# The second reading of x by two row gathers issued from GpSimd instead of two transfers issued from SyncE

## The chip, the core and the metric

The kernel runs on one core of a Trainium2 chip. A core has five engines with queues of their own: TensorE (PE in the profile, PEld for its weight loads), VectorE (DVE), ScalarE (ACT), GpSimd (POOL) and SyncE (SP), which here only issues DMAs (SPq). They share an on-chip memory (SBUF) and an accumulator memory (PSUM), and they order each other by semaphores. The metric is the device time of one execution in microseconds (us); lower is better.

## The reference

x is 8 x 1024 x 256, float32. Four blocks are added onto it, each behind a layer norm.

```python
x = x + attn_a(_layernorm(x), ...)   # gated linear attention (16 heads), then an MLP 256-512-256
x = x + ffn(_layernorm(x), ...)      # 8 experts 256x256, top two weighted
x = x + attn_b(_layernorm(x), ...)   # recurrence h = tanh(x_t B + h A^T), 16 wide, over 1024 steps
x = x + ffn(_layernorm(x), ...)      # the same expert layer again

def attn_a(x, ...):
    h = _ln(x, ln_w, ln_b)
    ...                               # o = gated linear attention of h, normed and gated
    x = x + o.reshape(Bb, Tt, HEADS * DV) @ Wo
    h2 = _ln(x, ln_w, ln_b)
    return x + jax.nn.gelu(h2 @ W1 + b1, approximate=False) @ W2 + b2
```

The raw x is wanted twice: once at the start, for the norms, and again later, for the normed x inside attn_a (`x` there) and for the outer `x +`.

## The kernel before, in words

Time is cut into 32 rounds of 32 steps (TS). One round holds 8 batch rows x 32 steps = 256 tokens, as two tiles of 128 partitions; a token's 256 numbers lie along the partition. Work on a round is spread over eight stages: in iteration `it` of the loop, stage k works on round it - k. Eight iterations are written out at the start, then a loop over `it` from 8 to 31, then seven more for the end. Each engine has its own program in the order written out by hand in its `body(it)`, and waits on semaphores; nothing is reordered at run time.

The names that matter. `xin` is the first reading of x (stage 0), `xag` the second (stage 2). From `xag` VectorE makes `xhat` (line 881), the normed x, one tile at a time, and GpSimd makes `res` = xag + b2 in stage 3 (line 485). When `res` of a round is done, `xag` may be overwritten. GpSimd then forms `state` (line 489), adds `xmid` to `res` (line 496), writes `elast` (line 499) and, from VectorE's moments `mv_f`, makes the reciprocal standard deviation `rf` (lines 401 and 403, a power). VectorE waits for `rf` in order to make `y` from `xmid` (line 881 too; one helper). Later GpSimd adds `part` and `acc` for the expert layer (lines 431 and 433).

The recurrence runs through all engines' programs: TensorE's step (line 1271, tile `ps<-hs,aT`), ScalarE's two tanh (lines 566 and 567), VectorE's `hs` (line 858), 32 times a round, interleaved with the other work.

SyncE's program in each iteration: the spreads of v and of the scores through DRAM (`vrow`, `vx`, `arow`, `atx`), then `xin` of a new round, then `xag`, then the store of a finished round. The second reading waits only for `res` of the round before, and stands behind the spreads in SyncE's queue.

Of the kernel before, what the change touches and what calls it, by code (L numbers as in the profile page):

```python
# [8 lines left out]
U32 = mybir.dt.uint32  # L9
ALU = mybir.AluOpType  # L10
# [3 lines left out]
P = 128  # L14
B, T, D = 8, 1024, 256
# [81 lines left out]
def build(nc, x, wts, out):  # L97
    ctx = ExitStack()
    with ctx:
# [5 lines left out]
        def sem(name):  # L105
            if name not in sems:
                sems[name] = ctx.enter_context(nc.semaphore(name))
            return sems[name]
# [131 lines left out]
        REST = {w: n + 1 for n, w in enumerate(("gate", "early", "scaled_out", "late", "recurrence", "experts0", "experts"))}  # L240
        recurrence_weights = [(a_raw[m * N:(m + 1) * N, n * N:(n + 1) * N], wts["A"]) for m in range(3) for n in range(3)]
        X_FIRST = 16 * TILES * (BQ - 1)
        GATE, EARLY, LATE = (16 * len(w) for w in (gate_weights, early_sync + early_scalar, late_sync + late_scalar))
        A_LOADED = 16 * len(recurrence_weights)

        def live(it, stage):

            return not isinstance(it, int) or 0 <= it - stage < ROUNDS
# [36 lines left out]
        def past(count):  # L285

            return max(count, 0) if isinstance(count, int) else count
# [18 lines left out]
        def load_first(eng, dst, i, name):  # L306
            for q in range(BQ):
                eng.dma_start(dst[q * TS:(q + 1) * TS, i, :], x[i * BQ + q, 0:TS, :]).then_inc(sem(name), 16)

        @block.sync  # L310
        def _(sp):
            def load_x(dst, n, name):
                for i in range(TILES):
                    sp.dma_start(dst[:, i, :], x[i * BQ:(i + 1) * BQ, bass.ds(n * TS, TS), :]).then_inc(sem(name), 16)

            def store(n):
                for i in range(TILES):
                    sp.dma_start(out[i * BQ:(i + 1) * BQ, bass.ds(n * TS, TS), :], m2.acc[:, i, :]).then_inc(sem("stored"), 16)

            load_first(sp, xin, 0, "x_loaded")  # L320
            for dst, src in early_sync:
                sp.dma_start(dst, src).then_inc(sem("early"), 16)
            for i in range(TILES):
                load_first(sp, xag, i, "x_again")
            sp.wait_ge(sem("pads_zero"), 1)
            sp.wait_ge(sem("early"), EARLY)
            for dst, src in late_scalar + late_sync[:6]:
                sp.dma_start(dst, src).then_inc(sem("late"), 16)
            sp.wait_ge(sem("spread_zero"), 1)

            def spread_v():
                for h in range(HQ):
                    cols = slice(h * J * DV, (h + 1) * J * DV)
                    sp.dma_start(vx[h * TS:(h + 1) * TS, :, h, :], vrow[:, :, cols].rearrange("b s c -> s b c")).then_inc(sem("v_spread"), 16)

            def spread_scores():
                for h in range(HQ):
                    sp.dma_start(atx[h * TS:(h + 1) * TS], arow[:, :, h, :].rearrange("b s c -> s b c")).then_inc(sem("att_spread"), 16)

            def body(it):  # L340
                c0, c2, c7 = (cnt(it, k) for k in (0, 2, 7))
                if live(it, 2):
                    spread, last, written = value(sp, c2), value(sp, c2 - 1), value(sp, c2 * 16)
                    sp.wait_ge(sem("pads_zero"), 1)
                    sp.wait_ge(sem("O11"), last)
                    sp.wait_ge(sem("vt1"), spread)
                    sp.wait_ge(sem("vt0"), spread)
                    sp.dma_start(vrow.rearrange("(i q) s c -> (q s) i c", q=BQ), vtok[:]).then_inc(sem("v_out"), 16)
                    sp.wait_ge(sem("pads_zero"), 1)
                    sp.wait_ge(sem("v_out"), written)  # L350
                    spread_v()
                    masked, kept = value(sp, 2 * c2), value(sp, c2 * 16)
                    sp.wait_ge(sem("pads_zero"), 1)
                    sp.wait_ge(sem("att"), masked)
                    sp.dma_start(arow.rearrange("(i q) s h c -> (q s) i (h c)", q=BQ), att[:].rearrange("p i h c -> p i (h c)")).then_inc(sem("att_out"), 16)
                    sp.wait_ge(sem("pads_zero"), 1)
                    sp.wait_ge(sem("att_out"), kept)
                    spread_scores()
                if live(it, 0) and not (isinstance(it, int) and it == 0):
                    sp.wait_ge(sem("y0"), past(TILES * (c0 - 1)))  # L360
                    load_x(xin, it, "x_loaded")
                if isinstance(it, int) and it == 1:
                    for dst, src in late_sync[6:]:
                        sp.dma_start(dst, src).then_inc(sem("late"), 16)
                    for dst, src in recurrence_weights:
                        sp.dma_start(dst, src).then_inc(sem("a_loaded"), 16)
                if isinstance(it, int) and it == 2:
                    sp.wait_ge(sem("weights_rest"), REST["late"])
                    sp.dma_start(stage[:].rearrange("p (c e d) -> p c e d", c=KC, e=E), wts["experts"]).then_inc(sem("experts"), 16)
                if live(it, 2) and not (isinstance(it, int) and it == 2):  # L370
                    sp.wait_ge(sem("res"), past(c2 - 1))
                    load_x(xag, it - 2, "x_again")
                if live(it, 7):
                    sp.wait_ge(sem("acc2"), c7 * VECTOR_GROUPS * 2)
                    store(it - 7)

            rounds(sp, body)
            sp.wait_ge(sem("stored"), 16 * TILES * ROUNDS)


        @block.gpsimd
        def _(pool):
# [12 lines left out]
            g.memset(state[:], 0.0).then_inc(sem("pads_zero"), 1)  # L395
            pool.wait_ge(sem("pads_zero"), 1)
            pool.wait_ge(sem("spread_zero"), 1)

            def rstd(mv, buf, name, count, shift=False):

                g.tensor_scalar(buf[:, 0, :], mv[:, :, 1], EPS, 1.0, ALU.add, ALU.mult).then_inc(sem(f"var_{name}"), 1)  # L401
                pool.wait_ge(sem(f"var_{name}"), count)
                g.tensor_tensor(buf[:, 1, :], buf[:, 0, :], mhalf[:, 0:TILES], ALU.pow).then_inc(sem(f"rstd_{name}"), 1)
                if shift:
                    pool.wait_ge(sem(f"rstd_{name}"), count)
                    g.tensor_tensor(buf[:, 0, :], buf[:, 1, :], mv[:, :, 0], ALU.mult).then_inc(sem(f"mr_{name}"), 1)
                    target = value(pool, count)
                    pool.wait_ge(sem("pads_zero"), 1)
                    pool.wait_ge(sem(f"mr_{name}"), target)
                    g.tensor_scalar(buf[:, 2, :], buf[:, 0, :], -1.0, 1.0, ALU.mult, ALU.mult).then_inc(sem(f"shift_{name}"), 1)  # L410
# [24 lines left out]
            def keep_norm(count):  # L435

                pool.wait_ge(sem("rstd_inner"), count)
                pool.wait_ge(sem("xhat"), past(TILES * (count - 1)))
                g.tensor_tensor(nrm[:, 1, :], ra[:, 1, :], one[:, 0:TILES], ALU.mult)
                g.tensor_tensor(nrm[:, 0, :], mv_a[:, :, 0], one[:, 0:TILES], ALU.mult).then_inc(sem("nrm"), 1)  # L440

            def gated(count):

# [4 lines left out]
            def body(it):  # L448
# [34 lines left out]
                if live(it, 3):  # L483
                    pool.wait_ge(sem("x1"), past(c3 - 1))
                    g.tensor_tensor(res[:], xag[:], b2[:].unsqueeze(1).broadcast_to([P, TILES, D]), ALU.add).then_inc(sem("res"), 1)
                if live(it, 2):
                    pool.wait_ge(sem("smid"), c2)
                    pool.wait_ge(sem("dstate"), c2)
                    g.tensor_tensor(state[:], smid[:], dstate[:], ALU.add).then_inc(sem("state"), 1)
# [10 lines left out]
                if live(it, 3) and not filling(it):  # L500
                    target = value(pool, c3)
                    pool.wait_ge(sem("pads_zero"), 1)
                    pool.wait_ge(sem("mv_f"), target)
                    rstd(mv_f, rf, "f", c3)
                if live(it, 4):
                    pool.wait_ge(sem("scaled1"), past((c4 - 1) * 2 * TILES + 2))
                    start_acc(m1, 0, c4)
# [315 lines left out]
        def _(dve):  # L823
# [131 lines left out]
            def body(it):  # L955
# [192 lines left out]
                    split_state(15, c5)  # L1148
                if live(it, 2):
                    dve.wait_ge(sem("nrm"), c2)  # L1150
                    dve.wait_ge(sem("x_again"), c2 * 16 * TILES + X_FIRST)
                    normed(xhat, xag, nrm[:, 0, :], nrm[:, 1, :], 0).then_inc(sem("xhat"), 1)
                if live(it, 3):
                    dve.wait_ge(sem("h2T0"), c3)
# [518 lines left out]
```

## Time and profile before

| | |
|---|---|
| time, median of 2 runs | 1697.11 us (1696.15 to 1698.06) |
| span of the profiled execution, first to last instruction | 1692.7 us |
| that execution's own time | not given apart from the two runs; its span is 4.4 us under their median |
| granted TensorE clock, mean over the span | 0.974 |
| busy: TensorE, VectorE, ScalarE, GpSimd | 94%, 75%, 62%, 49% |
| one full round in the middle | 48.6 us |
| DMA | 48 GB/s over the span |

A row of a timeline has: start, duration, engine, line, operation, tile written <- tiles read, shapes, count; in brackets the idle time of the engine just before it and what ended that. Rows that follow each other closely on an engine are merged (x2, x4). Busy shares are averages: where an engine's idle time lies in a round is seen only in its timeline.

### The profile page before, as it was taken

To read this page: it belongs to the slowest core of one execution; us is meant where nothing else is said; L and a number is where in the kernel's file an instruction comes from. 1 tells how busy PE (TensorE), PEld (TensorE's weight loads), DVE (VectorE), ACT (ScalarE), POOL (GpSimd) and SP (SyncE) were. 2 spreads that over 40 slices of the span, in tenths; PEclk is the share of its full clock that TensorE was granted. 3 is DMA by queue.
4 is the path that set the end of the run, shared out by engine and by line. 5 is a ranking of instruction groups with operands and counts; after the bars stand their busy time and mean duration, and the time that the engine had idled before them with its cause. 6 is when DMAs were issued, how large, how long until landed. Compare 5 with 4: busy or idle time off the path is not lost.

```text
span 1692.7 us, 51627 instructions
## 1 busy us (share of the span) xinstructions
PE 1591.6 (94%) x16840; PEld 1324.5 (78%) x16840; DVE 1274.3 (75%) x4556; ACT 1051.2 (62%) x3851; POOL 823.1 (49%) x1294
## 2 busy tenths in 40 slices
PE   4588999999999999999999999999999999998866
PEld 3477888888888888888888888888888888887654
DVE  4566777887788778787888787887888877876544
ACT  4656666666766666666666666666666667655431
POOL 3554454554555455545454554454545545543211
PEclk7799999999999999999999999999999999999978
DMA  5211111111111111011111111111111111110000
GB/s 151 84 57 45 52 58 58 42 39 43 43 56 56 56 51 43 31 52 47 56 56 56 46 42 35 50 50 56 56 56 43 37 44 44 52 52 8 7 7 13
DMA packets 117250, 81.49 MB, mean 48 GB/s; under 512 B 42016, under 2 KB 108224, under 8 KB 117056
## 3 DMA queue, kind: packets, MB, share of 16 engines
q1 hardware_dynamic: 116208, 80.10, 15.4%
q8 instruction: 38, 0.62, 0.2%
q10 hardware_dynamic: 976, 0.54, 0.1%
q14 instruction: 28, 0.23, 0.0%
HBM read 47.06 MB, written 33.55 MB: 48 GB/s over the span
## 4 chain that ended last, share of the span: by engine, by line
PE 82%; DVE 6%; issue 3%; DMA 3%; ACT 2%; SPq 2%; POOL 1%; ACTq 0%; DVEq 0%; POOLq 0%
PE ps L1254 62%; PE ps L1260 4%; PE ps L1271 4%; PE ps L1285 2%; PE ps L1301 2%; PE ps L1442 2%; PE ps L1331 2%; DMA xag<-in_x 2%; PE ps L1321 2%; PE ps L1312 1%; DVE hs L858 1%; DVE att L947 1%; DVE dstate L1075 1%; PE ps L1292 1%; DMA arow<-att 1%
## 5 line engine op out<-in xcount | busy, mean ns | idle before, releaser
L1254 PE MATMUL ps<-we,yT 128*128 128x512 f32 x3072 | 824.5, 411 | 0.3 <-DVE h2Ts L953 0.3
L1254 PEld LDWEIGHTS ps<-we,yT 128*128 128x128 f32 x3072 | 546.5, 191 | 100.9 <-issue 1.1
L566 ACT ACTIVATE h_lead<-ps 48x8 fp32r<-48x8 f32 x1024 | 172.4, 168 | 443.8 <-PE ps L1271 430.3
L858 DVE SCALAR_TENSOR_TENSOR hs<-ps,cst,h_lead 48x8 fp32r<-48x8 f32 x1024 | 224.7, 219 | 223.8 <-ACT ps L567 216.1
L1271 PEld LDWEIGHTS ps<-hs,aT 128*128 128x128 f32 x1024 | 195.1, 191 | 126.4 <-DVE hs L858 99.1
L1271 PE MATMUL ps<-hs,aT 128*128 128x8 f32 x1024 | 215.9, 211 | 39.7 <-DVE hs L858 38.3
L890 DVE SCALAR_TENSOR_TENSOR stage<-ps,coef,stage 128x256 f32<-128x256 f32 x384 | 183.1, 477 | 13.8 <-POOL stage L433 5.0
L890 DVE SCALAR_TENSOR_TENSOR acc<-ps,coef,acc 128x256 f32<-128x256 f32 x384 | 181.7, 473 | 6.6 <-POOL acc L433 2.7
L518 POOL TENSOR_TENSOR orstd<-omean,mhalf 128x32 f32<-128x32 f32 x32 | 174.6, 5455 | 0.2
L567 ACT ACTIVATE ps<-ps 48x8 f32<-48x8 f32 x1024 | 162.8, 159 | 0.0
L431 POOL TENSOR_TENSOR part<-part 128x256 f32<-128x256 f32 x64 | 46.9, 732 | 204.2 <-ACT part L584 201.8
L431 POOL TENSOR_TENSOR stage<-stage 128x256 f32<-128x256 f32 x64 | 47.8, 746 | 187.7 <-ACT stage L584 187.7
L1254 PE MATMUL ps<-h2Ts,wa 128*128 128x256 f32 x768 | 106.9, 289 | 3.7 <-DVE h2Ts L953 3.7
L1254 PE MATMUL ps<-wa,gTs 128*128 128x256 f32 x768 | 108.1, 291 | 0.7 <-DVE gTs L953 0.6
L1254 PE MATMUL ps<-wa,hTs 128*128 128x512 f32 x384 | 103.3, 406 | 0.0
L1254 PEld LDWEIGHTS ps<-wa,gTs 128*128 128x128 f32 x768 | 96.0, 191 | 7.0 <-issue 6.0
L1254 PEld LDWEIGHTS ps<-h2Ts,wa 128*128 128x128 f32 x768 | 95.8, 191 | 5.4 <-DVE h2Ts L953 3.9
L512 POOL TENSOR_SCALAR omean<-oss 128x32 f32<-128x32 f32 x32 | 8.9, 277 | 178.5 <-DVE oss L1172 178.5
L575 ACT ACTIVATE ps<-ps,lnb,lnw 128x256 f32<-128x256 f32 x128 | 67.2, 529 | 30.5 <-PE ps L1260 30.5
L1254 PEld LDWEIGHTS ps<-wa,hTs 128*128 128x128 f32 x384 | 67.6, 188 | 14.1
L401 POOL TENSOR_SCALAR ra<-mv_a 128x2 f32<-128x2 f32 x32 | 6.1, 191 | 145.0 <-DVE mv_a L877 145.0
L606 ACT ACTIVATE qx<-qt,cst 128x256 f32<-128x256 f32 x128 | 64.4, 505 | 1.4 <-DVE qt L977 1.4
(184 smaller groups left out, 3200.4 us busy)
## 6 DMA issues: line engine op xcount, KB each, us to landing
arow<-att SPq DMA_DIRECT2D x32, 512.0 KB, 2.8
atx<-arow SPq DMA_DIRECT2D x128, 128.0 KB, 2.8
vrow<-vtok SPq DMA_DIRECT2D x32, 256.0 KB, 2.1
vx<-vrow SPq DMA_DIRECT2D x128, 64.0 KB, 2.0
out<-stage SPq DMA_DIRECT2D x64, 128.0 KB
xin<-in_x SPq DMA_DIRECT2D x62, 128.0 KB
xag<-in_x SPq DMA_DIRECT2D x62, 128.0 KB
stage<-in_experts SPq DMA_DIRECT2D x1, 2048.0 KB, 9.5
```

The costliest lines, as they stand in the source:

```text
L431: g.tensor_tensor(m.part[:, i, 0, :], m.part[:, i, 0, :], m.part[:, i, 1, :], ALU.add).then_inc(sem(f"part{m.s}"), 1)
L518: g.tensor_tensor(orstd[:], omean[:], mhalf[:], ALU.pow).then_inc(sem("orstd"), 1)
L566: a.activation(h_lead[:], ps[0:NB, BANK["RB"], k * B:(k + 1) * B], ACT.Tanh)
L567: a.activation(h_whole, ps[0:NB, BANK["RB"], k * B:(k + 1) * B], ACT.Tanh).then_inc(sem("rnn_tanh"), 1)
L575: a.activation(ps[:, bank, c * TOK:(c + 1) * TOK], ps[:, bank, c * TOK:(c + 1) * TOK], ACT.Identity, bias=lnb[:, c:c + 1], scale=lnw[:, c: ...
L606: return a.activation(qx[:, h, :, :], bt(qt[:]), ACT.Identity, scale=headmask[:, h:h + 1])
L858: v.scalar_tensor_tensor(hs[0:NB, :, k], h_whole, keeps_rest, h_lead[:].bitcast(F32), ALU.mult, ALU.subtract).then_inc(sem("rnn_h"), 1)
L890: v.scalar_tensor_tensor(m.acc[:, i, :], ps[:, bank, half * D:(half + 1) * D], m.coef[:, i, e:e + 1], m.acc[:, i, :], ALU.mult, ALU.add).t ...
L1254: ins = t.matmul(dst, left(lp, c), right(rp, c), start=(n == 1), stop=(n == 3 * chunks))
L1260: ins = t.transpose(ps[:, dst_bank, c * TOK + i * P:c * TOK + (i + 1) * P], src[:, i, c * P:(c + 1) * P], ident)
L1271: return t.matmul(ps[0:NP, BANK["RB"], k * B:(k + 1) * B], aT[:], hs[:, :, (k - 1) % TS], start=False, stop=True, skip_group_check=True)
L1285: ins = t.matmul(ps[ROUTED * g:ROUTED * (g + 1), bank, 0:TOK], rw[:, c, :], m.yT[:, part, c, :].bitcast(F32), start=True, stop=True, skip_ ...
```

## The change

SyncE no longer reads `xag`, neither in its loop (two transfers an iteration) nor at the start (eight transfers of 32 rows for round 0). GpSimd gets the numbers of the 2 x 128 rows of round 0 in a small tile `row` (four iotas; a fifth fills `row[:, 1]` with 32). In iterations 2 to 33 it issues two indirect DMAs, each gathering 128 rows of 1 KB of x by the numbers in one column of `row`; then, some instructions on, it waits for both to have landed and adds 32 to the row numbers. VectorE's wait for the landing counts from the new number.

```diff
@@ setup
+        rows_x = x.rearrange("b t d -> (b t) d")
+        row = sb("row", [P, 2, TILES], U32)
@@ SyncE
-            for i in range(TILES):
-                load_first(sp, xag, i, "x_again")
...
-                if live(it, 2) and not (isinstance(it, int) and it == 2):
-                    sp.wait_ge(sem("res"), past(c2 - 1))
-                    load_x(xag, it - 2, "x_again")
@@ GpSimd, start
+            for q in range(BQ):
+                ins = g.iota(row[q * TS:(q + 1) * TS, 0, :], [[BQ * T, TILES]], base=q * T, channel_multiplier=1)
+            ins.then_inc(sem("rows_first"), 1)
+            pool.wait_ge(sem("rows_first"), 1)
+            g.iota(row[:, 1, :], [[0, TILES]], base=TS, channel_multiplier=0).then_inc(sem("row"), 1)
...
+            def read_again(count):
+                target = value(pool, past(count - 1))
+                pool.wait_ge(sem("pads_zero"), 1)
+                pool.wait_ge(sem("res"), target)
+                pool.wait_ge(sem("row"), count)
+                for i in range(TILES):
+                    g.indirect_dma_start(xag[:, i, :], None, rows_x, bass.IndirectOffsetOnAxis(ap=row[:, 0, i:i + 1], axis=0)).then_inc(sem("x_again"), 16)
+
+            def next_rows(count):
+                target = value(pool, count * 16 * TILES)
+                pool.wait_ge(sem("pads_zero"), 1)
+                pool.wait_ge(sem("x_again"), target)
+                g.tensor_tensor(row[:, 0], row[:, 0], row[:, 1], ALU.add).then_inc(sem("row"), 1)
@@ GpSimd, body: between res and state
                     g.tensor_tensor(res[:], xag[:], b2[:].unsqueeze(1).broadcast_to([P, TILES, D]), ALU.add).then_inc(sem("res"), 1)
                 if live(it, 2):
+                    read_again(c2)
+                if live(it, 2):
                     pool.wait_ge(sem("smid"), c2)
@@ GpSimd, body: between rf and the start of acc
                     rstd(mv_f, rf, "f", c3)
+                if live(it, 2):
+                    next_rows(c2)
                 if live(it, 4):
@@ VectorE
-                    dve.wait_ge(sem("x_again"), c2 * 16 * TILES + X_FIRST)
+                    dve.wait_ge(sem("x_again"), c2 * 16 * TILES)
                     normed(xhat, xag, nrm[:, 0, :], nrm[:, 1, :], 0).then_inc(sem("xhat"), 1)
```

The order on GpSimd in the loop, from `r` of the expert layer to the first `acc`, before:

```order
L410 TENSOR_SCALAR r<-r 128x2
L485 TENSOR_TENSOR res<-xag,b 128x512
L489 TENSOR_TENSOR state<-smid,dstate 128x512
L496 TENSOR_TENSOR res<-res,xmid 128x512
L499 TENSOR_TENSOR elast<-eq,one 128x8
L401 TENSOR_SCALAR rf<-mv_f 128x2
L403 TENSOR_TENSOR rf<-rf,mhalf 128x2
L506 ISA
L431 TENSOR_TENSOR part<-part 128x256
```

and the same place now:

```order
L412 TENSOR_SCALAR r<-r 128x2
L503 TENSOR_TENSOR res<-xag,b 128x512
L451 DMA xag<-in_x,row 128x256 x2
L509 TENSOR_TENSOR state<-smid,dstate 128x512
L516 TENSOR_TENSOR res<-res,xmid 128x512
L519 TENSOR_TENSOR elast<-eq,one 128x8
L403 TENSOR_SCALAR rf<-mv_f 128x2
L405 TENSOR_TENSOR rf<-rf,mhalf 128x2
L294 ISA
L458 TENSOR_TENSOR row<-row 128x2
L528 ISA
L433 TENSOR_TENSOR part<-part 128x256
```

Two DMAs stand between `res` and `state`, and the addition to `row` between `rf` and `part`. (ISA rows are register work and waits.)

The end of SyncE's loop, from the score spread on, before:

```order
L338 DMA atx<-arow 32x8x128 x4
L360 REGISTER_ALU
L314 ISA
L314 DMA xin<-in_x 128x1x256
L314 ISA
L314 DMA xin<-in_x 128x1x256
L314 ISA
L314 DMA xag<-in_x 128x1x256
L314 ISA
L314 DMA xag<-in_x 128x1x256
L374 ISA
L318 ISA
```

and now:

```order
L338 DMA atx<-arow 32x8x128 x4
L360 REGISTER_ALU
L316 ISA
L316 DMA xin<-in_x 128x1x256
L316 ISA
L316 DMA xin<-in_x 128x1x256
L371 ISA
L320 ISA
```

The two `xag` transfers and their address work are gone; the stores (line 318, now 320) follow `xin` directly.

## Rows read from the trace of the kernel before

**Rows 1.** The page: busy time by engine, and the chain by engine

```profile
PE 1591.6 (94%) x16840; PEld 1324.5 (78%) x16840; DVE 1274.3 (75%) x4556; ACT 1051.2 (62%) x3851; POOL 823.1 (49%) x1294
...
PE 82%; DVE 6%; issue 3%; DMA 3%; ACT 2%; SPq 2%; POOL 1%; ACTq 0%; DVEq 0%; POOLq 0%
```

**Rows 2.** Windows, one full round: length, busy time by engine, clock, DMA

```profile
800.00:848.60 48.60, 48.37 (x528) 40.57 (x527) 39.24 (x143) 32.36 (x122) 25.50 (x41) 1.00 0.16 49
```

**Rows 3.** Timeline of GpSimd in a full round

```profile
813.29 0.19 POOL L410 TENSOR_SCALAR r<-r 128x2 f32<-128x2 f32 x1 [0.16 <-POOL r L406]
...
815.13 1.31 POOL L485 TENSOR_TENSOR res<-xag,b 128x512 f32<-128x512 f32 x1
816.39 1.51 POOL L489 TENSOR_TENSOR state<-smid,dstate 128x512 f32<-128x512 f32 x1
...
819.38 0.19 POOL L401 TENSOR_SCALAR rf<-mv_f 128x2 f32<-128x2 f32 x1
819.65 0.71 POOL L403 TENSOR_TENSOR rf<-rf,mhalf 128x2 f32<-128x2 f32 x1
826.10 0.72 POOL L431 TENSOR_TENSOR part<-part 128x256 f32<-128x256 f32 x1 [5.74 <-ACT part L584]
```

**Rows 4.** Timeline of all engines in the same round

```profile
818.74 0.23 DVE L877 BATCH_NORM_AGGREGATE mv_f<-st_f 128x2 f32<-128x6 f32 x2
...
820.39 0.41 DVE L881 TENSOR_SCALAR y<-xmid,mv_f,rf 128x256 f32<-128x256 f32 x1 [0.51 <-POOL rf L403]
...
820.72 0.22 DVE L858 SCALAR_TENSOR_TENSOR hs<-ps,cst,h_lead 48x8 fp32r<-48x8 f32 x1
...
821.21 0.19 PEld L1271 LDWEIGHTS ps<-hs,aT 128*128 128x128 f32 x1
...
822.63 0.20 DVE L858 SCALAR_TENSOR_TENSOR hs<-ps,cst,h_lead 48x8 fp32r<-48x8 f32 x1
...
822.89 0.19 PEld L1271 LDWEIGHTS ps<-hs,aT 128*128 128x128 f32 x1 [0.34 <-DVE hs L858]
```

**Rows 5.** Tile xag: duration ns min/median/max, first and last; waits for it

```profile
L314 SPq DMA_DIRECT2D xag<-in_x x62: 531/548/615, 64.4 to 1502.1; - x62
...
  DMA xag<-in_x: 8.6, 9
```

**Rows 6.** Timeline of SyncE's queue in the same round

```profile
822.34 1.30 SPq L314 DMA_DIRECT2D xag<-in_x  x2
```

**Rows 7.** Timeline of GpSimd in iterations 2 to 5

```profile
31.28 3.71 POOL L489 TENSOR_TENSOR state<-smid,dstate 128x512 f32<-128x512 f32 x1 [3.78 <-DVE dstate L1075]
...
58.86 1.31 POOL L489 TENSOR_TENSOR state<-smid,dstate 128x512 f32<-128x512 f32 x1 [3.04 <-DVE dstate L1075]
...
98.40 0.19 POOL L401 TENSOR_SCALAR rf<-mv_f 128x2 f32<-128x2 f32 x1 [1.09 <-DVE mv_f L877]
...
136.99 0.19 POOL L401 TENSOR_SCALAR rf<-mv_f 128x2 f32<-128x2 f32 x1 [0.23 <-DVE mv_f L877]
```

**Rows 8.** Timeline of all engines and SyncE's queue where xag comes late, iterations 3 and 7

```profile
64.41 1.11 SPq L314 DMA_DIRECT2D xag<-in_x  x2
...
71.61 0.41 DVE L881 TENSOR_SCALAR xhat<-xag,nrm 128x256 f32<-128x256 f32 x1 [5.26 <-DMA xag<-in_x]
...
72.68 2.72 PE L1254 MATMUL ps<-h2Ts,wa 128*128 128x256 f32 x11 [3.67 <-DVE h2Ts L953]
...
235.72 1.11 SPq L314 DMA_DIRECT2D xag<-in_x  x2
...
244.04 0.41 DVE L881 TENSOR_SCALAR xhat<-xag,nrm 128x256 f32<-128x256 f32 x1 [0.85 <-DMA xag<-in_x]
```

**Rows 9.** Timeline of VectorE: iteration 2, and the full round

```profile
31.06 2.81 DVE L841 TENSOR_TENSOR wa<-stage,wa 128x2560 fp32r<-128x2560 f32 x1
...
816.37 0.40 DVE L881 TENSOR_SCALAR y<-xin,mv_a,ra 128x256 f32<-128x256 f32 x1
...
829.23 0.41 DVE L881 TENSOR_SCALAR xhat<-xag,nrm 128x256 f32<-128x256 f32 x1
```

## The prediction

> **What bounds the kernel now.** I read the page first: engine shares and the chain [rows 1]. TensorE is busy 94% of the span and stands for 82% of the chain that ended last. Then the stages by windows [rows 2]: in a full round of 48.60 us TensorE is busy 48.37 at a granted clock of 1.00, VectorE 39.24, GpSimd 25.50. So a round is as long as TensorE's own list, and TensorE has nothing in reserve with which to win back a stall. GpSimd at half load looks roomy, and that is the trap: the question is where in the round its idle time lies. I read that in its timeline [rows 3]. After the late start of the `ra` work it runs without a gap through res, state, res + xmid, elast and rf, until 820.36, and only then rests 5.74 us until 826.10. The new gathers are put inside the packed stretch (between L485 and L489), the new wait and addition into the idle gap.
>
> Next, who waits for the end of the packed stretch [rows 4]. VectorE has mv_f ready at 818.97; GpSimd begins rf at 819.38, because it is behind, and VectorE's y (line 881) has stood idle for 0.51 us when rf comes. Queued behind y on VectorE is the next hs of the recurrence (820.72), and behind a stretch without a gap the one after (822.63 to 822.83). TensorE loads for that step at 822.89, having waited 0.34 for it. The first hs has about 0.2 us to spare (820.94 against 821.21), the second about none. So each microsecond added on GpSimd between res and rf moves y, then hs, then TensorE, nearly one for one, in each full round.
>
> **The change, part by part.**
>
> *Removed from SyncE:* two transfers a round, 1.30 us of issue for the pair at 822.34 [rows 6], 0.548 us the median of one [rows 5]. SyncE then waits for later work; only the stores stand behind, and nobody on the chip waits for those before the next round. Worth nothing. The eight first transfers at the start are likewise followed by a wait for weights. Nothing; their traffic could bring up to 1 us by my estimate, which I leave out.
>
> *Earlier arrival.* The rows now start off on the gather's own issue, about 6 us before SyncE's turn. VectorE waited 8.6 us in nine places for them [rows 5]. The largest was 5.26 at 71.61, where TensorE stood still 3.67 behind it [rows 8]; the issue had ended at 65.52, so the landing took 6.1 us. At 244.04 it took 7.2 us from the issue's end (236.83) and the wait was 0.85. I count 3.7 for the first and half of the other 3.3 us, since a short wait on VectorE is partly hidden: 3.7 + 1.7 = **5.4 us gained**.
>
> *Added on GpSimd in the packed stretch:* the wait on its own res, which no longer lets the next instruction start under it, and two indirect DMAs. The wait: 0.16 us, as for r behind r [rows 3]. One indirect DMA is shown nowhere in this trace. Bound from below: SyncE's issue, 0.55 [rows 5] (a dearer unit can't be argued to be cheaper than the one made for it). From above: 3.71, the longest hold of a GpSimd instruction in this stretch of the program [rows 7], when it had to share with VectorE. I take the lower row plus one small software-bound GpSimd instruction, the two-element power of 0.71 [rows 3]: 0.55 + 0.71 = 1.26, rounded to 1.25, since the engine must do the issue and first work out addresses. I stay near the lower end because 128 rows of 1 KB are few, and because the 3.71 has a partner on VectorE that the gathers lack. So the pair holds GpSimd 0.16 + 2 x 1.25 = **2.66 us** (ends: 1.26 and 7.58).
>
> The Trainium skill (DMA: Bandwidth & Descriptors, Latency and other measured facts) gives about 1 us until the first byte of a DMA whose descriptors GpSimd writes, and about 0.6 for SyncE's kind. No row here shows that; by 1.0 us for each the pair would be 2.16 and the total 1755.
>
> *How many times:* 32 pairs, iterations 2 to 33. GpSimd idles 3.78 us before state in iteration 2 and 3.04 in iteration 3 [rows 7], which covers the pair. In iteration 4 it idles 1.09 before rf, so 1.57 remain; in iteration 5, 0.23, so 2.43 remain. Iterations 6 to 33 pay all: 28 x 2.66 = 74.5. Together 78.5.
>
> *Added in the gap:* the wait for the landing and the 128x2 addition (about 0.2 us, as the other 128x2 instructions). GpSimd gets there at 820.36 + 2.66 = 823.0; the gathers were issued by 819.1 and with the slower landing above, 7.2 us, are there at 826.3. Behind the wait is `part` (826.10, now 828.8, because its input from ScalarE slides with the round). Hidden with 2.5 us to spare; xhat, at 829.23 [rows 9] and now 831.9, has more. The iotas at the start fall in an idle stretch of GpSimd. Nothing.
>
> Sum: 78.5 - 5.4 = +73.1 us. The profiled execution's span is 1692.7, so 1765.8; the timed runs' median lies 4.4 above that span, so **1770 us**, +4.3%. Per round: 48.6 becomes about 51.2.
>
> **The rivals.**
>
> *GpSimd is not held.* If the descriptors are made while GpSimd's next instruction runs, state begins at 816.4 as before, and only the earlier arrival remains: 1697.1 - 5.4 = 1692. For it: SyncE's issue instructions are not counted as work, and GpSimd's queue is separate from its arithmetic. Against it: SyncE's own issues stand one behind the other, 0.65 us apart. It decides below 0.19 us for the pair (5.4 / 28). Chance 0.08, all within 2%.
>
> *A cheap issue.* At SyncE's price the pair is 1.26: iterations 4 and 5 pay 0.17 and 1.03, the others 35.3; with the gain 1697.1 + 36.5 - 5.4 = 1728. Chance of below 1735: 0.06, mostly within 2%.
>
> *VectorE locks GpSimd out.* In iteration 2 state took 3.71 instead of 1.31 beside VectorE's 2.81 us subtraction of two SBUF operands [rows 7, 9]. If each gather were held like that, the pair is 7.58 and the sum 3.8 + 4.5 + 6.5 + 7.4 + 212.2 - 5.4 = +229: 1926. Against it: from 816.4 to 819 VectorE's one instruction with all data in SBUF and a large output is y, 0.40 us [rows 9]; with it alongside, state took 1.51, 0.2 more. The Trainium skill (SBUF — State Buffer, the box on VectorE blocking a DMA) has this very rule: while VectorE runs a two-port operation, GpSimd cannot write descriptors, and a 620 ns DMA takes 3100. By that figure the total would be near 1887 if each gather met one; the trace shows one short candidate a round. Chance 0.06.
>
> *The landing is late.* The gathers share the DMA engines with SyncE's spreads. `part` moves only if landing takes over 9.7 us from the issue (828.8 - 819.1). At 12 us each of 28 rounds pays 2.3 more: 1834. Chance 0.04.
>
> The forecast, GpSimd held for 1.5 to 4.5 us a round and TensorE paying it, has 0.76.
>
> **How the numbers follow.** 1770 is the forecast's. The cost of a gather is the wide term: 0.66 us each gives 1735, 2.2 each gives 1830. The range 1735 to 1830 takes in the forecast, which carries 0.76, and part of the late landing. What lies below is the two cheap rivals (0.14, less what misses the edge), above it the lock. A measurement here tells 2% from no change: under 1663 or over 1731. Faster: 0.02, since no term is near 34 us of gain. Same: 0.08 and most of 0.06, 0.12. Slower: 0.86.
>
> **What would show each step.** Right: between res and state on GpSimd a gap or instructions of 2.3 to 3.3 us; VectorE's y waiting for rf about 3.2 instead of 0.51 in rounds 6 to 33; TensorE idle about 2.6 once a round, behind hs, and its granted clock still 1.00 there; the round 51.2; no wait of xhat for xag; `part` still waiting for ScalarE. Wrong: state beginning 0.2 us after res (first rival); DVE idle time over 5 us before y (lock); `part` waiting for GpSimd's row addition (landing). The step most likely to be off in size is the 1.25; in kind, that VectorE passes all of it on.

## The result, and the profile after

The changed kernel took **1796.18 us** (median of 2 runs, 1795.63 to 1796.74) against 1697.11 before: ratio 1.0599, 95% interval 1.0574 to 1.0624. The forecast was 1770, range 1735 to 1830.

From the page after the change: busy times, the gathers' queue, and one group of instructions (busy us, mean ns of one | idle before them and what ended it).

```profile
PE 1627.2 (91%) x16840; PEld 1348.2 (75%) x16840; DVE 1275.6 (71%) x4556; ACT 1053.7 (59%) x3851; POOL 892.6 (50%) x1395
q0 software_dynamic: 3072, 8.39, 1.8%
L1276 PE MATMUL ps<-we,yT 128*128 128x512 f32 x3072 | 850.2, 421 | 0.6 <-DVE hTs L975 0.6
```

Against [rows 1], VectorE's and ScalarE's work is the same within 3 us. GpSimd has 69.5 us more, nearly all of it the gathers. TensorE has 35.6 us more with the same 16840 instructions: the product we x yT takes 421 ns where it took 411. Work that has not changed and takes longer points at TensorE's clock.

GpSimd's timeline in a full round (start us, duration us, engine line op, [idle before it]), the counterpart of [rows 3]:

```profile
859.89 1.30 POOL L503 TENSOR_TENSOR res<-xag,b 128x512 f32<-128x512 f32 x1
861.99 1.09 POOL L451 DMA_INDIRECT xag<-in_x,row  x1 [0.80 <-issue]
863.39 0.95 POOL L451 DMA_INDIRECT xag<-in_x,row  x1 [0.30 <-issue]
864.36 1.30 POOL L509 TENSOR_TENSOR state<-smid,dstate 128x512 f32<-128x512 f32 x1
865.61 1.27 POOL L516 TENSOR_TENSOR res<-res,xmid 128x512 f32<-128x512 f32 x1
867.12 0.19 POOL L403 TENSOR_SCALAR rf<-mv_f 128x2 f32<-128x2 f32 x1
867.39 0.72 POOL L405 TENSOR_TENSOR rf<-rf,mhalf 128x2 f32<-128x2 f32 x1
868.11 0.19 POOL L458 TENSOR_TENSOR row<-row 128x2 uint32<-128x2 uint32 x1
875.03 0.73 POOL L433 TENSOR_TENSOR part<-part 128x256 f32<-128x256 f32 x1 [6.73 <-ACT part L606]
```

Between the end of res (861.19) and state (864.36) lie 3.2 us: 0.80 before the first gather, 1.09, 0.30, 0.95. Everything below is later by that, and the gap before `part` is no shorter than before (6.73 against 5.74): the hold was put where GpSimd had no time, and the time it had is unused.

The same round on VectorE and TensorE, the counterpart of [rows 4]:

```profile
868.15 0.41 DVE L903 TENSOR_SCALAR y<-xmid,mv_f,rf 128x256 f32<-128x256 f32 x1 [3.48 <-POOL rf L405]
868.75 0.19 PEld L1293 LDWEIGHTS ps<-hs,aT 128*128 128x128 f32 x1 [2.73 <-DVE hs L880]
870.65 0.29 PEld L1293 LDWEIGHTS ps<-hs,aT 128*128 128x128 f32 x1 [0.57 <-DVE hs L880]
870.89 2.91 PE L1276 MATMUL ps<-we,yT 128*128 128x512 f32 x6
```

VectorE waits 3.48 for rf (0.51 before), then TensorE 2.73 for hs. The last row is the second loss: six products take 2.91, where the same six take 1.64 to 1.72 at a granted clock of 1.00. Windows of the same stretch (length; busy PE, PEld, DVE, ACT, POOL; granted clock; DMA share; GB/s):

```profile
866.00:868.00 2.00, 0.26 (x3) 0.02 (x1) 0.00 (x0) 0.07 (x1) 1.83 (x4) 1.00 0.82 151
868.00:870.00 2.00, 1.25 (x6) 1.07 (x7) 1.85 (x6) 0.23 (x2) 0.29 (x2) 1.00 0.27 96
870.00:872.00 2.00, 1.96 (x7) 1.24 (x6) 1.58 (x17) 0.34 (x3) 0.00 (x0) 0.57 0.23 66
872.00:874.00 2.00, 2.00 (x8) 1.57 (x7) 0.72 (x7) 0.13 (x2) 0.00 (x0) 0.57 0.26 80
874.00:876.00 2.00, 2.00 (x29) 1.61 (x30) 1.04 (x3) 1.33 (x7) 0.89 (x2) 1.00 0.00 1
```

TensorE is nearly idle from 866 to 868 and works again from 868.7. The granted clock then falls: it is 0.57 in each of two windows of 2 us, which is 1.00 for a part of them and the lower level, 0.50, for about 3.4 us (0.43 x 4 / 0.5). This round lasts 52.97 us from res to res; the one ahead of it, with the clock at 1.00 throughout, 51.64; the next, where the clock falls just as TensorE starts again, 52.60. The pattern 51.6, 52.9, 52.6 repeats through most of the kernel, while TensorE's wait is 2.73 to 2.80 in all of these rounds.

The waits (engine line <- releaser: us in total, times, longest), and then the gathers by their tile (least, median and largest ns, and the time to landing):

```profile
DVE y L903 <- POOL rf L405: 106.6, 32, 3.6
PE ps L1293 <- DVE hs L880: 106.8, 108, 2.6
```

```profile
L451 POOL DMA_INDIRECT xag<-in_x,row x64: 945/1021/1325, 28.2 to 1598.4; - x64
DMA to landing us min/median/max: 2.8/3.1/4.4
```

Before, the first two were 18.1 and 38.3 us. Nobody waits for xag any more.

**The account.** res of iteration 6 starts at 179.67 (179.63 before): ahead of it nothing is lost on balance. The next 28 rounds take 1464.7 us instead of 1361.6, +103.1. In the middle of the kernel a round without a fall of the clock has +3.03; 28 times that is 84.8. In 18 of the 28 rounds the clock falls around TensorE's restart, and these have 21.5 more (about 1.0 each, and 2.5 in each of the two in which it stays down twice as long). The first three rounds (iterations 6 to 8) grow by 3.2 less than 3 x 3.03; two of the waits for xag before lay there (0.85 each, at 244.04 and 294.13), but no run separates what that is worth. The rest of the span gives back 1.3. 84.8 + 21.5 - 3.2 - 1.3 = +101.8, the spans' difference (1794.5 to 1692.7).

### The profile page after: what moved, and what is told of

It reads as the page before. It is cut to its first block and busy times, and to the rows that moved or that the text cites. A ratio compares the mean times of both kernels' runs of the same rounds, so it can differ in the third digit from the quotient of the medians.

```text
span 1794.5 us, 51650 instructions
## 1 busy us (share of the span) xinstructions
PE 1627.2 (91%) x16840; PEld 1348.2 (75%) x16840; DVE 1275.6 (71%) x4556; ACT 1053.7 (59%) x3851; POOL 892.6 (50%) x1395
## 5 line engine op out<-in xcount | busy, mean ns | idle before, releaser
L1276 PE MATMUL ps<-we,yT 128*128 128x512 f32 x3072 | 850.2, 421 | 0.6 <-DVE hTs L975 0.6
L1276 PEld LDWEIGHTS ps<-we,yT 128*128 128x128 f32 x3072 | 563.3, 197 | 109.0 <-issue 1.5
L1293 PEld LDWEIGHTS ps<-hs,aT 128*128 128x128 f32 x1024 | 198.9, 194 | 199.4 <-DVE hs L880 170.2
L903 DVE TENSOR_SCALAR y<-xmid,mv_f,rf 128x256 f32<-128x256 f32 x64 | 27.7, 435 | 106.6 <-POOL rf L405 106.6
L451 POOL DMA_INDIRECT xag<-in_x,row x64 | 65.6, 1025 | 35.1 <-issue 35.1
```

What stands on the lines that cost most here:

```text
L451: g.indirect_dma_start(xag[:, i, :], None, rows_x, bass.IndirectOffsetOnAxis(ap=row[:, 0, i:i + 1], axis=0)).then_inc(sem("x_again"), 16)
L903: return v.tensor_scalar(dst[:, i, :], src[:, i, :], mean[:, i:i + 1], scale[:, i:i + 1], ALU.subtract, ALU.mult)
L1276: ins = t.matmul(dst, left(lp, c), right(rp, c), start=(n == 1), stop=(n == 3 * chunks))
L1293: return t.matmul(ps[0:NP, BANK["RB"], k * B:(k + 1) * B], aT[:], hs[:, :, (k - 1) % TS], start=False, stop=True, skip_group_check=True)
```

## The experiments

Each ratio is against runs of the kernel before on the same chip, with its 95% interval. Theory: the pair's hold of GpSimd passes into the round through rf, y and hs, and its stall also costs clock. The rivals are given with each.

**1. The gathers alone, moved behind rf** (e1_gap). `next_rows` goes in front of the wait for `oss`.

```
-                if live(it, 2): read_again(c2)       # between res and state
...
-                if live(it, 2): next_rows(c2)        # behind rf
+                if live(it, 2): read_again(c2)       # behind rf
...
+                if live(it, 2): next_rows(c2)        # ahead of omean
```

> The changed kernel with the two gathers moved behind rf, into GpSimd's idle gap, and the addition to row moved behind the first acc. Theory (place): the pair holds GpSimd for about 3.2 us wherever it stands, but the gap of 5.7 us before part covers it, so the round is again 48.6 us, TensorE's granted clock stays at 1.00 in the middle, and the time is 1690 to 1700. Rival (price): the gathers cost by themselves, through their traffic or their descriptors, and the time stays above 1750.

Measured 1692.39 us, ratio 0.9979 [0.9964, 0.9993]. The same 64 gathers; the round is back at 48.7, the clock in the middle at 1.00, y's waits at 18.0 us. GpSimd's timeline in that kernel:

```profile
866.35 0.71 POOL L405 TENSOR_TENSOR rf<-rf,mhalf 128x2 f32<-128x2 f32 x1
867.24 1.09 POOL L451 DMA_INDIRECT xag<-in_x,row  x1 [0.19 <-issue]
868.64 0.95 POOL L451 DMA_INDIRECT xag<-in_x,row  x1 [0.30 <-issue]
872.88 0.72 POOL L433 TENSOR_TENSOR part<-part 128x256 f32<-128x256 f32 x1 [3.29 <-ACT part L606]
```

The gathers take 2.5 us out of the idle gap ahead of `part`, and 3.29 us of it are left. The gathers, their traffic and the missing work of SyncE cost nothing by themselves; only their place does.

**2. The hold without a gather** (e2_hold4): the kernel before, with four two-element powers between res and state.

```
+                    for k in range(4):
+                        g.tensor_tensor(held[:, k, :], one[:, 0:2], mhalf[:, 0:2], ALU.pow)
```

> The kernel before (SyncE reads xag) with four two-element powers on scratch data put between res and state, 4 x 0.78 = 3.1 us of GpSimd and no DMA. Theory (place): the same as the change without its earlier arrival, a round of 51.7 with some rounds at 52.8 where TensorE's clock falls to the lower level, about 1800. Rival (price): GpSimd's time there is mostly covered, below 1720.

Measured 1773.81, ratio 1.0465 [1.0434, 1.0496]. The powers hold GpSimd 2.92 us; the round is 51.30 (+2.70). y waits 3.21, TensorE's weight load 2.46 and its matmul 2.22. Of the 24 rounds of iterations 9 to 32 the clock falls in four, and they last 52.1 to 52.7. No DMA was changed: time on GpSimd alone brings four fifths of the loss. The missing fifth is the subject of experiment 5.

**3. One gather instead of two** (e3_one); SyncE reads tile 1.

```
-                for i in range(TILES):
+                for i in range(1):
                     g.indirect_dma_start(xag[:, i, :], ...)
```

> The changed kernel with one gather for tile 0 and SyncE's transfer for tile 1. The hold falls from 3.2 to about 1.9 us (0.8 before the first gather, 1.1 for it). If each microsecond reaches TensorE and the shorter stall leaves the clock at its upper level: 1697 + 28 x 1.8 + 3 = 1750 or a little less with the earlier arrival. If the clock falls as often as in the change: 1775. If the price is not in the hold: near 1796.

Measured 1736.93, ratio 1.0237 [1.0206, 1.0267]; round 50.37 (+1.77), clock 1.00 in every round from iteration 9 on. GpSimd's timeline:

```profile
834.57 1.30 POOL L507 TENSOR_TENSOR res<-xag,b 128x512 f32<-128x512 f32 x1
836.67 1.09 POOL L455 DMA_INDIRECT xag<-in_x,row  x1 [0.80 <-POOL res L507]
837.79 1.28 POOL L513 TENSOR_TENSOR state<-smid,dstate 128x512 f32<-128x512 f32 x1
```

The hold is 1.92 (0.80 + 1.09), so of the pair's 3.17 the second gather costs 1.25 and the first 1.92: the 0.80 is paid once, with one gather as with two. The round grows by 0.15 less than the hold, because state, which starts later and no longer beside a y, takes 1.28 where it took 1.51 (the same with the pair: hold 3.17, round +3.03).

**4. SyncE's read brought forward, no gather** (e4_sp_early): its two transfers go ahead of its wait for the scores' copy.

> The kernel before with SyncE's xag transfers moved ahead of its wait for arow, so ahead of the score spread: the earlier arrival alone, nothing on GpSimd. I put 5.4 us of gain on it: 1692. If the extra traffic delays arow and with it atx: 1697 or more. The rival that the earlier arrival is worth nothing gives 1697.

Measured 1692.65, ratio 0.9981 [0.9967, 0.9995], and no wait for xag. The early arrival alone is worth about 0.2%, as in experiment 1, and it needs no GpSimd.

**5. A hold of the gathers' length, without DMA** (e9_hold32): as 2, with one 48-element product behind the powers.

> The kernel before (SyncE reads x again, no gather) with dummy work on GpSimd between res and state: four powers of two elements, 2.92 us in the earlier experiment, and one product of 48 elements, an estimate of 0.3 us more; a scratch result that nobody reads. The hold is then as long as the pair of gathers (3.2 us), without any DMA. Theory A (the length of TensorE's stall alone lowers its clock, as the 2.50 us wait for hs after the change did and the 2.22 us wait of the shorter hold did not): most rounds go on at 0.57 for some us and last 52.5 to 52.9, the others 51.6; time 1785 to 1800. Theory B (the gathers' traffic or their queue has to do with the clock's fall): the rounds are 51.6 throughout and the time is 1697 + 28 x 3.0 = about 1781 or less.

Measured 1794.65, ratio 1.0580 [1.0562, 1.0598], the changed kernel's time. The timeline:

```profile
859.55 2.87 POOL L490 TENSOR_TENSOR held<-one,mhalf 128x2 f32<-128x2 f32 x4
862.39 0.26 POOL L491 TENSOR_TENSOR more<-one 128x48 f32<-128x48 f32 x1
862.61 1.29 POOL L495 TENSOR_TENSOR state<-smid,dstate 128x512 f32<-128x512 f32 x1
...
866.99 0.19 PEld L1277 LDWEIGHTS ps<-hs,aT 128*128 128x128 f32 x1 [2.67 <-DVE hs L864]
```

```profile
868.00:870.00 2.00, 1.93 (x7) 1.30 (x6) 1.61 (x15) 0.34 (x3) 0.00 (x0) 0.64 0.25 89
870.00:872.00 2.00, 2.00 (x7) 1.52 (x6) 0.93 (x8) 0.00 (x0) 0.00 (x0) 0.51 0.26 92
```

(Windows of the same stretch, columns as above.) The weight load waits 2.67 us, the clock falls, and the rounds repeat 51.6, 52.9, 52.6, as with the gathers. Theory A holds: the clock falls behind the stall without any gather. Of the same 24 rounds it falls in four at 2.46 us of that wait (experiment 2) and in 16 at 2.67. The length is not all of it: with the same 2.67 us the clock falls in two rounds and stays up in the third. What decides that is not shown.

**6. A longer hold** (e10_hold6): six powers, 4.3 us. The theories differ on the clock.

> The kernel before with six powers of two elements between res and state, a hold of 6 x 0.73 = 4.4 us and no DMA. If the hold passes into the round at full price and nothing else happens, the rounds are 48.6 + 4.2 = 52.8 and the time 1697 + 28 x 4.2 = about 1815. Theory A (a longer stall of TensorE also lowers its clock): the wait of TensorE for hs is about 3.7 us, the clock falls in all or nearly all rounds, a round lasts 54 or more and the time is 1840 to 1860. Theory B (the fall belongs to the gathers): 1815, clock 1.00.

Measured 1864.13, ratio 1.0967 [1.094, 1.0994]. The round is 54.6 nearly every time. y starts 9.29 us after res, 4.0 later than before; in experiment 2 it started 2.7 later and the round grew by 2.70. By the hold alone the round would so be about 52.6, and some 2.0 us are clock. The timeline, then the windows from where TensorE starts again:

```profile
903.03 0.37 PE L1275 MATMUL ps<-hs,aT 128*128 128x8 f32 x1 [3.52 <-DVE hs L862]
```

```profile
902.00:904.00 2.00, 0.97 (x3) 0.88 (x4) 1.57 (x5) 0.23 (x2) 0.39 (x1) 0.50 0.27 94
904.00:906.00 2.00, 2.00 (x7) 1.52 (x6) 1.61 (x15) 0.22 (x1) 0.00 (x0) 0.50 0.27 96
906.00:908.00 2.00, 2.00 (x7) 1.61 (x6) 1.04 (x8) 0.23 (x2) 0.00 (x0) 0.50 0.27 96
```

The clock is down when TensorE starts again at 903.0 and stays down to the end of these windows, for 5 us of its work.

**7. The gathers one instruction later** (e8_after_state): behind state.

```
-                if live(it, 2): read_again(c2)       # ahead of state
                 g.tensor_tensor(state[:], ...)
+                    read_again(c2)
```

> The changed kernel with the two gathers one instruction later, behind state and ahead of res+xmid, so that res has long ended when the first gather waits for it. Theory A (of the 0.80 us ahead of the first gather about 0.6 is the wait for GpSimd's own res to write out and signal): the gap is 0.2, as in the experiment with the gathers in the gap, the hold 0.19 + 1.09 + 0.30 + 0.95 = 2.5, round 48.6 + 2.4 = 51.0, clock 1.00, time 1697 + 28 x 2.4 - 5 = about 1760. Theory B (the first gather after a long operation pays 0.8 whatever it waits for): hold 3.2, rounds and time as in the changed kernel, about 1796.

Measured 1765.81, ratio 1.0404 [1.0386, 1.0421]; round 51.22. The clock falls in two of the 24 rounds. GpSimd's timeline:

```profile
847.61 1.49 POOL L507 TENSOR_TENSOR state<-smid,dstate 128x512 f32<-128x512 f32 x1
849.28 1.09 POOL L451 DMA_INDIRECT xag<-in_x,row  x1 [0.17 <-issue]
850.68 0.95 POOL L451 DMA_INDIRECT xag<-in_x,row  x1 [0.30 <-issue]
```

The gap is 0.17 where it was 0.80. So 0.63 us of the hold was the wait for GpSimd's own res, the instruction just ahead. 0.2 of that is lost again, since state is now beside VectorE's y and takes 1.49. Moving the pair by one instruction saves 0.4 us a round and, since the weight load's wait falls to 2.36, nearly all of the clock's share too: 30 us in all, with nothing else changed.

**8. Plain transfers from GpSimd's queue** (e5_direct) in place of the gathers, no row numbers.

> Two plain transfers from GpSimd's queue at the place of the two gathers, no row numbers. Theory A (what holds GpSimd is that it writes the descriptors of an indirect transfer itself, 1.0 us each): a plain transfer takes well under 1 us of the engine; the hold is the wait for res of 0.6 and 0.1 to 0.5 for each, in all 1 to 1.6, time 1725 to 1742. Theory B (any transfer from GpSimd's queue costs about 1 us of the engine): hold 2.7 to 3.2, time 1770 to 1800.

Measured 1753.75, ratio 1.0335 [1.0317, 1.0352]: between the two expectations. GpSimd's timeline:

```profile
844.62 1.45 POOL L487 DMA_DIRECT2D xag<-in_x  x2 [0.74 <-POOL res L482]
846.09 1.29 POOL L491 TENSOR_TENSOR state<-smid,dstate 128x512 f32<-128x512 f32 x1
```

A plain transfer holds the engine 0.73 us, a gather 1.02. Theory A was right on the order, wrong on "well under 1": most of the price is paid for issuing from GpSimd at all. The round is 50.66, but for one of the profiled execution that lasts 57.95:

```profile
792.97 0.69 POOL L487 DMA_DIRECT2D xag<-in_x  x1 [5.55 <-issue]
```

There GpSimd stands 5.55 us between the two transfers, TensorE's weight load waits 7.31 and the clock falls too. The cause is open; that round alone is 7.3 us of the profiled execution's loss.

**9. rf directly behind the gathers** (e12_rf_next), ahead of state, **10. rf ahead of res + xmid in the kernel before** (e11_rf_first), **11. that with the gathers in the gap** (e13_both).

```
+                if live(it, 3) and not filling(it):
+                    ...
+                    rstd(mv_f, rf, "f", c3)          # 9: ahead of state; 10, 11: ahead of res + xmid
...
-                if live(it, 3) and not filling(it):  # the same, behind elast
```

> The changed kernel with both gathers where they are, but in full rounds rf directly behind them, ahead of state, res+xmid and elast. Theory A (what costs is only that rf stands behind the hold; mv_f is ready 2.3 us after res has ended, so most of a hold of 3.2 us can be covered): in the times of the round before, res ends at 816.4, the gathers at 819.6, rf at 820.55, y starts at 820.7 instead of 820.39: round 48.9, clock 1.00, time 1697 + 28 x 0.3 = 1700 to 1710. Theory B (the gathers disturb more than GpSimd's order: the port, the transfers' traffic, or state and res+xmid that now end 2.9 us later are waited for): rounds of 50 or more, 1740 to 1800.

> The kernel before, without gathers, with rf one place earlier in full rounds: behind state, ahead of res+xmid and elast. mv_f is ready at 818.97, rf ends now at 820.36 and would end at about 820.0. Theory A (each us by which rf is earlier or later is a us of the round, in this direction too): round 48.6 - 0.4 = 48.2, time 1697 - 30 x 0.35 = about 1686. Theory B (TensorE's 0.34 us stall behind y is all that can be saved, or its other work ends at the same time): 0 to -0.2 us a round, 1690 to 1697.

> The gathers in the gap behind rf (which alone gave 0.9979 of the time before) and rf ahead of res+xmid. If the two gains add up: 0.2% and what the other kernel of this batch shows, about 1683. If the gathers' place now collides with the later res+xmid and elast: no better than the one without gathers.

Measured: 1739.76, ratio 1.0262 [1.0239, 1.0285]; 1718.57, ratio 1.0127 [1.0103, 1.0151]; 1713.27, ratio 1.0111 [1.009, 1.0133]. None brought the gain that was meant: 9 came out at the lower edge of Theory B (round 50.3), 10 above both theories, and 11 no better than 10, as in its second case. In 11, GpSimd's and VectorE's timeline:

```profile
874.28 0.71 POOL L405 TENSOR_TENSOR rf<-rf,mhalf 128x2 f32<-128x2 f32 x1
874.96 1.30 POOL L519 TENSOR_TENSOR res<-res,xmid 128x512 f32<-128x512 f32 x1
875.02 1.39 DVE L903 TENSOR_SCALAR y<-xmid,mv_f,rf 128x256 f32<-128x256 f32 x1 [0.26 <-POOL rf L405]
```

y starts 5.02 us after res, earlier than the 5.26 of before [rows 3, 4], as meant. But it takes 1.39 us instead of 0.41, and ends just after GpSimd's res + xmid, which had started 0.06 ahead of it. Gain 0.2, loss 0.97: round 49.35. In 9, y starts 5.55 us after res (the 0.3 us late that was expected), then both y are stretched beside state and res + xmid:

```profile
841.69 1.37 DVE L903 TENSOR_SCALAR y<-xmid,mv_f,rf 128x256 f32<-128x256 f32 x1 [0.79 <-POOL rf L405]
843.51 0.84 DVE L903 TENSOR_SCALAR y<-xmid,mv_f,rf 128x256 f32<-128x256 f32 x1
```

48.6 + 0.3 + 0.96 + 0.44 = 50.3, as measured, with the clock at 1.00. In 9 to 11 the order freed a GpSimd product to start at the very moment at which rf freed y.

**12. The gathers as cover for y** (e14_cover): rf, the gathers, then res + xmid.

> Like the last kernel with both edits, but the two gathers stand between rf and res+xmid, so that the two y on VectorE run beside the gathers and not beside a product of 512 elements on GpSimd. Theory A (in the last three kernels y took 1.38 us instead of 0.41 because GpSimd's res+xmid started 0.06 us ahead of it and VectorE's y can only run beside it to its end; a gather does no such thing): y takes 0.4 to 0.5 us and starts 0.2 us earlier after res than in the kernel before, the round lasts 48.6 - 0.2 = 48.4, time 0.993 to 0.997 of before. Theory B (rf ahead of res+xmid costs 0.8 us a round for another reason, such as res+xmid or elast being late, now by 2.5 us more): rounds of 49.4 or longer, 1.011 of before or more.

Measured 1714.97, ratio 1.0108 [1.0087, 1.0129]: Theory B's time. But its timeline:

```profile
875.51 0.48 DVE L903 TENSOR_SCALAR y<-xmid,mv_f,rf 128x256 f32<-128x256 f32 x1 [0.26 <-POOL rf L405]
875.66 1.09 POOL L451 DMA_INDIRECT xag<-in_x,row  x1 [0.19 <-issue]
876.44 0.40 DVE L903 TENSOR_SCALAR y<-xmid,mv_f,rf 128x256 f32<-128x256 f32 x1
...
878.02 1.30 POOL L521 TENSOR_TENSOR res<-res,xmid 128x512 f32<-128x512 f32 x1
878.30 1.07 DVE L935 TENSOR_TENSOR sub<-lm 128x20 f32<-128x20 f32 x1
```

Both y are short again, so Theory A's mechanism held for y. res + xmid now meets another VectorE instruction, the 20-element `sub` of two SBUF operands: 1.07 us instead of 0.16, again until GpSimd's product ends. Over the kernel `sub` takes 40.9 us where it took 10.2, 0.96 us a round. What stands behind it (the softmax, then the next hs, for which TensorE waits 1.15) pays for it. The loss moved from one VectorE instruction to the next. That this is all of the loss is read from the timeline; a place for res + xmid that meets neither was not tried.

No version beat experiments 1 and 4, 0.2% under the kernel before.

## Why the prediction was right, and where it was off

- **Who pays** (right). The packed stretch from res to rf passed every hold on to y, hs and TensorE: holds of 1.92, 2.92 and 3.17 us gave rounds of +1.77, +2.70 and +3.03. Removing the pair from the stretch gave all of it back (experiment 1).
- **The price of a gather** (a little high): 1.25 taken, 1.02 measured, within the ends 0.55 and 3.71. SyncE's row plus a small instruction was a fair neighbour. The other figure in the prediction, about 1 us by the Trainium skill (DMA: Bandwidth & Descriptors, Latency and other measured facts), is a time to the first byte, which no run here shows. That the instruction held the engine for 1.02 is the same size and does not confirm it. The total of 1755 was too low for the two reasons that follow.
- **The gaps** (the mis-sized term). I took 0.16 for the wait on res, from a two-element instruction that waits for another. The wait for the 512-element res came to 0.80 before the first gather, and 0.30 stood between the two: 1.10 instead of 0.16. The pair is 3.17 instead of 2.66. Of these 0.51 us 0.14 come back through the shorter state, which the prediction did not count, so it is +0.37 us a round in the clean rounds (3.03 against 2.66), some 10 us in all.
- **The clock** (the step that failed). I had it stay at 1.00 with TensorE idle for 2.6 us. TensorE idled 2.50 (its weight load waited 2.73), and in 18 of 28 rounds the clock fell: 21.5 us. Experiments 2, 5 and 6 show that the stall brings this without a gather, and the more often the longer it is. It is the largest term that the forecast lacked; the range held the result because it was wide for the price of a gather, not because it allowed for the clock.
- **The start and the end**: +4.0 for iterations 4 and 5 and -5.4 for the early arrival were predicted, -1.4 together. Measured were 0.0 ahead of iteration 6, -3.2 in iterations 6 to 8 and -1.3 at the end, -4.5 together. By experiment 4 the early arrival is worth 3.2 us (0.9 to 5.6 by its interval) of the 5.4 I had counted.
- **The sum again**: 1770.2 + 10.3 (gaps) + 21.5 (clock) - 3.1 (start and end) - 2.7 = 1796.2, as measured. The 2.7 is because the timed median lies 1.7 above the profiled span here, not 4.4.
- **Hidden parts** (right): nobody waited for the landing (3.1 us, at most 4.4, against the 7.2 I had allowed) nor for the addition to `row` (0.19 us in a gap of 6.7). SyncE's freed time was worth nothing.
- **The rivals.** "GpSimd is not held" and "a cheap issue" fell with the timeline. The late landing fell with the landing times. The lock did not happen in the changed kernel: no long VectorE instruction with all data in SBUF runs beside the pair. A gather can be held, though. In experiments 1 and 12 the one gather that met VectorE's 2.27 us product of two SBUF operands took 2.31 and 2.87 us, and both ended 0.82 us after that product (2.32 and 0.83 in experiment 11). The rule that the prediction quotes is about two-port operations; this product is the other kind, with two SBUF operands.

## What to carry to other kernels

Cost an instruction by its place, not by its engine's idle share: the same two gathers were worth +6% in a packed stretch that another engine waits for, and -0.2% five instructions later. A wait for the instruction just ahead leaves a gap on the engine; one independent instruction between the two took away 0.63 us of gap. And where a stall of TensorE comes near the 2.5 us from which the clock was lost here, price the clock beside the stall. When you reorder GpSimd, look up what VectorE starts at the same moment: an instruction of 0.16 us can last as long as the GpSimd product it meets.

## What the runs showed of the hardware

- **A stall of a few us costs TensorE its clock, the more often the longer it is.** In the 24 rounds of iterations 9 to 32 the weight load's wait was 1.5 us in experiment 3 and the clock never fell; at 2.36 (experiment 7) it fell in 2 of the 24, at 2.46 (experiment 2) in 4, at 2.67 (experiment 5) in 16, at 2.73 to 2.80 (the changed kernel) in 17, and at 3.5 to 3.8 (experiment 6) in all. It fell to 0.50, its lower level (1.2 GHz of 2.4), for about 3.4 us in the changed kernel. Such a fall cost about 1.0 us there and 2.0 in experiment 6, beside the stall. Why it comes in some rounds and not in others with the same wait is open.
- **Some instructions of GpSimd and VectorE wait each other out.** y (0.41 to 1.39 us) and `sub` (0.16 to 1.07) lasted until 0.15 and 0.05 us after a 512-element instruction of GpSimd that had started 0.06 and 0.28 us ahead of them. Others did not: the two FIND_INDEX8 ahead of `sub` took their usual 0.16 beside the same one. In the other order GpSimd's state takes 1.5 instead of 1.3 beside y. The Trainium skill (SBUF — State Buffer, SBUF: two separate sides) states this: the one that starts first has the shared ports for its whole instruction and the other is blocked, whether VectorE's is of the two-port kind or has two SBUF inputs. The trace agrees for `sub`, which has two SBUF inputs, and for y if it is of the two-port kind, which no row shows.
- **A gather is milder.** Where y starts 0.15 us ahead of a gather (experiments 1 and 12), either y takes 0.48 instead of 0.41 and the gather its usual 1.09, or y takes 0.41 and the gather 1.23.
- **Prices on GpSimd**: a gather of 128 rows of 1 KB 1.02 us in the median (1.09 the first of a pair, 0.95 the second, at most 1.33), its landing 3.1 us from the issue; a plain transfer of the same tile 0.73; 0.30 between two gathers; ahead of the first 0.17 to 0.19 without a wait and 0.80 behind its own 512-element instruction.
